# Cross attention: the first query tile is transposed into the bank of the transposed probabilities

## The chip, the cores and the metric

The kernel runs on one core of one Trainium2 chip. The metric is the time of one execution on the device in microseconds. It is given as the median of several runs; the trace comes from one more execution, which was recorded.

## What is computed

One decoder block in float32 on 32 sequences of 64 tokens with 512 features: layer norm and causal self attention, layer norm and cross attention to a context of the same size, layer norm and a feed-forward part with a latent branch, each with its residual. The part that matters here is cross attention:

```python
# cross attention, H = 32 query heads, KVH = 8 key heads, HD = 128, 32 sequences of 64 tokens
q = (hidden_states @ Wq.T).reshape(bsz, q_len, H, HD).transpose(0, 2, 1, 3)
k = (cross_attention_states @ Wk.T).reshape(bsz, kv_len, KVH, HD).transpose(0, 2, 1, 3)
v = (cross_attention_states @ Wv.T).reshape(bsz, kv_len, KVH, HD).transpose(0, 2, 1, 3)
q = _rmsnorm(q, q_norm_w)
k = jnp.repeat(k, GROUPS, axis=1)
v = jnp.repeat(v, GROUPS, axis=1)
k = _rmsnorm(k, k_norm_w)
scores = jnp.einsum('bhqd,bhkd->bhqk', q, k) * scale
scores = scores + attention_mask[:, :, :, :kv_len]
probs = jax.nn.softmax(scores.astype(jnp.float32), axis=-1).astype(q.dtype)
out = jnp.einsum('bhqk,bhkd->bhqd', probs, v)
...
x = x + _L0_attn_ref(_layernorm(x, axis=-1), ...)
x = x + _L0_xattn_ref(_layernorm(x, axis=-1), ctx_4096, mask_1x1xSxS2_ff0, ...)
x = x + _L0_ffn_ref(_layernorm(x, axis=-1), ...)
```

## The kernel before

**Tiling and stages.** The batch is worked off in two halves of 1024 tokens (16 sequences). Each half goes through self attention, cross attention and the feed-forward part. Products of float32 matrices are made from three products of a high and a low part (`split_mm`, lines 358 to 360: hi x hi, hi x lo, lo x hi), so every matrix that is multiplied is first split: ScalarE makes the high part, VectorE or GpSimd the rest.

Cross attention runs over eight turns, one for each key head with its four query heads (`REP` = 4), and in each turn over four chunks of 256 tokens (`CHUNKS` = 4). A turn is one pass of a loop with a register on every engine; the last turn of a half is written out, interleaved with the start of the feed-forward part (`last_turn_and_ffn`). There are 32 chunks in a half and 64 in all.

**What sets the order.** Each engine has its own list of instructions, written out by hand; they meet only at semaphores. `slot(place, k)` on TensorE is one chunk's worth of work, staggered over three chunks: the key and value projection of chunk k + 2 (`project_chunk_kv`, 24 matmuls of 256 columns), the scores of chunk k + 1 (`scores2`), the query projection of chunk k + 2 (`project_chunk_q`, 2 x 12 matmuls of 512 columns), the first output projection of chunk k, the transposed probabilities of chunk k + 1 (`transpose_probs`, into the bank `pt`), the second output projection, the values product of chunk k + 1 (`values2`), and the transposes of keys and queries of chunk k + 2 (`transpose_chunk`). ScalarE's slot follows the same order: copies of keys and values, exponentials, copies of the queries, `evacuate_probs` (line 733: `pt` to `probt`), `transposed_chunk` (lines 846 to 856), and the copy of the values product (`outputs_hi`, line 861). In one chunk of four, two pieces of the next output weights are split between `transposed_chunk` and `outputs_hi` (line 721, and line 1358 on GpSimd); other pieces are split elsewhere in two of the slots.

**The accumulator banks.** PSUM has eight banks here: `acc0` and `acc1`, `sc` for the scores, `pt` for the transposed probabilities, two of `ot` for the values product, `y0` and `y1` for the output projection. The two banks of `acc` are handed out by a running number n: use n goes to bank n % 2. `acc_bank(at, n)` (line 362) waits on TensorE until the use before it of that bank has been read out (`acc_free0` or `acc_free1`), and the last matmul of a use counts up `acc_rdy`, for which the reader waits. A chunk k has six uses, 6k to 6k + 5: keys and values, the two query projections, the transposed keys (`C_KT` = 3), and the two transposed query tiles (`C_QT` = 4 and 5).

`transpose_chunk` (line 539) is ten transposes of 128 x 128: two of the keys (line 544, `acc<-ident,kv`) and four for each query tile (`transpose_tile`, line 376, `acc<-ident,qb`; `qb` is the buffer that holds `qraw` and `q2t`). ScalarE copies the keys with the norm's weights (line 850, `kt<-acc`), then each query tile (line 855, `qb<-acc`). `scores2` waits for both query copies. In the profile a transpose's weight load is an LDWEIGHTS on PEld, and the transpose itself a MATMUL on PE. `scale_chunk` (lines 1087 and 1090 on VectorE) writes the normalised keys and queries that are transposed, after GpSimd's inverse roots (line 1362).

Of the kernel before, what the change touches and what calls it, by code (L numbers as in the profile page):

```python
# [33 lines left out]
CHUNKS = NT // 2  # L34
TURN = 6 * CHUNKS
ACC1 = 4 * NT + 6
# [6 lines left out]
PIECES = [(W_KV, 512), (W_KV + 512, 512), (W_Q, 1024), (W_Q + 1024, 1024), (W_O, 1024), (W_O + 1024, 1024)]  # L43
N_PIECES = 6 + 6 * NG + 8


# [53 lines left out]
def decoder_block(nc, x_in, ctx_in, mask_in, w_self, w_cross, qn_in, kn_in, w_ffn,  # L100
                  f1g_in, expt_in, fc2_in, gamma_in, beta_in, out):
    with ExitStack() as stack:
# [98 lines left out]
        k_sum = count("k_sum", 2, 0, CHUNKS, 0)  # L201
        qk_ve, qk_rs, qk_nrm = (count(n, 0, 0, CHUNKS, 0) for n in ("qk_ve", "qk_rs", "qk_nrm"))
        kbd_done = count("kbd_done", 0, NSEQ, 0, 0)
        vbd_done = count("vbd_done", 0, NSEQ, 0, 0)
# [19 lines left out]
        def use(place, k, j):  # L224


            if k == 0 and j < 3:
                return Place(1, place.half).at, A1[("ckv", "cq0", "cq1")[j]]
            return place.at, 6 * k + j

# [125 lines left out]
        def _(pe):  # L356
# [5 lines left out]
            def acc_bank(at, n):  # L362

                pe.wait_ge(acc_free[n % 2].sem, at(acc_free[n % 2], n // 2))
                return acc[n % 2]
# [173 lines left out]
            def transpose_chunk(place, k):  # L539
                at = place.at  # L540
                pe.wait_ge(qk_nrm.sem, at(qk_nrm, k + 1))
                to = acc_bank(at, 6 * k + C_KT)
                for t in range(2):
                    ins = nc.tensor.transpose(to[:, t * P:(t + 1) * P], kv[:, 2 * (k % CHUNKS) + t, 0:P], ident[:])  # L544
                ins.then_inc(acc_rdy.sem, 1)
                for t in range(2):
                    transpose_tile(at, 6 * k + C_QT + t, qraw[:, 2 * (k % 2) + t].rearrange("p h d -> p (h d)"))

            def scores2(place, k):
                at = place.at  # L550
                evacuated(pe, at, 6 * k + C_QT)
                evacuated(pe, at, 6 * k + C_QT + 1)
                pe.wait_ge(s_add.sem, at(s_add, k))
# [162 lines left out]
        def _(act):  # L716
# [129 lines left out]
            def transposed_chunk(at, k):  # L846
                n = 6 * k + C_KT
                c = k % CHUNKS
                act.wait_ge(acc_rdy.sem, at(acc_rdy, n + 1))
                nc.scalar.mul(kt[:, c * 2 * P:(c + 1) * 2 * P], acc[n % 2][:, 0:2 * P], qkn[:, 2:3]  # L850
                              ).then_inc(acc_free[n % 2].sem, 1)
                for t in range(2):
                    n = 6 * k + C_QT + t
                    act.wait_ge(acc_rdy.sem, at(acc_rdy, n + 1))
                    nc.scalar.copy(q2t[:, k % 2, t], acc[n % 2][:].rearrange("p (h b q) -> p b h q", h=REP, b=2)
                                   ).then_inc(acc_free[n % 2].sem, 1)

# [9 lines left out]
            def slot(place, k, front=True, mid=True, next_group=True):  # L867
# [3 lines left out]
                if next_group and k == 1:  # L871
                    act.wait_ge(acc_rdy.sem, at(acc_rdy, 6 * 3 + C_KV + 1))
                    split_piece(place, 6)
                    split_piece(place, 7)
# [5 lines left out]
                if next_group and k == 1:  # L880
                    act.wait_ge(acc_rdy.sem, at(acc_rdy, 6 * 3 + C_Q + 2))
                    split_piece(place, 8)
# [22 lines left out]
            def last_turn_and_ffn(half):  # L905
# [27 lines left out]
                queries(turn, 3, 0)  # L933
                act.wait_ge(acc_rdy.sem, turn.at(acc_rdy, 6 * 3 + C_KV + 1))
                split_piece(place, 0)
                queries(turn, 3, 1)
                evacuate_probs(turn.at, 2, 0)
                act.wait_ge(acc_rdy.sem, turn.at(acc_rdy, 6 * 3 + C_Q + 2))
                split_piece(place, 1)
# [618 lines left out]
```

## Time and profile before

| | us |
|---|---|
| median of 3 runs | 1846.23 |
| lowest and highest | 1844.5, 1850.87 |
| the profiled execution | 1853.32 |
| its span, first to last instruction | 1851.6 |
| TensorE matmuls busy | 1733.9 (94%) |
| TensorE weight loads busy | 1397.1 (75%) |
| VectorE, ScalarE, GpSimd busy | 941.9, 751.8, 650.7 |

The mean granted clock of TensorE over the span is 0.961. Busy time is the union of an engine's instructions. Matmuls overlap with each other in the records, and a weight load runs while the matmul before it does; so the start times of the weight loads tell more exactly than the busy share when TensorE went on. The profile counts time from the start of the span; cross attention with full slots lies between 234 and 787 us for the first half of the batch, and some 915 us later for the second.

### The profile page before, as it was taken

To read this page: it belongs to the slowest core of one execution; us is meant where nothing else is said; L and a number is where in the kernel's file an instruction comes from. 1 tells how busy PE (TensorE), PEld (TensorE's weight loads), DVE (VectorE), ACT (ScalarE), POOL (GpSimd) and SP (SyncE) were. 2 spreads that over 40 slices of the span, in tenths; PEclk is the share of its full clock that TensorE was granted. 3 is DMA by queue.
4 is the path that set the end of the run, shared out by engine and by line. 5 is a ranking of instruction groups with operands and counts; after the bars stand their busy time and mean duration, and the time that the engine had idled before them with its cause. 6 is when DMAs were issued, how large, how long until landed. Compare 5 with 4: busy or idle time off the path is not lost.

```text
span 1851.6 us, 29634 instructions
## 1 busy us (share of the span) xinstructions
PE 1733.9 (94%) x11352; PEld 1397.1 (75%) x11352; DVE 941.9 (51%) x1657; ACT 751.8 (41%) x1332; POOL 650.7 (35%) x511
## 2 busy tenths in 40 slices
PE   2989899999999999989949998999999999999898
PEld 1745678888888888878937557888888888887797
DVE  3169544444545544474450894545444445456654
ACT  1267444444443434431223763443434444434221
POOL 2188323242323332451012972322332322324410
PEclk8889999999999999999968998999999999999999
DMA  4110010110101101110041100101101101011100
GB/s 154 41 40 18 18 40 19 40 40 17 57 17 40 57 17 45 35 46 18 18 147 31 38 7 18 41 17 40 57 17 40 40 23 51 23 39 47 35 24 23
DMA packets 25871, 70.92 MB, mean 38 GB/s; under 512 B 3152, under 2 KB 3152, under 8 KB 25808
## 3 DMA queue, kind: packets, MB, share of 16 engines
q1 hardware_dynamic: 25808, 70.05, 12.2%
q8 instruction: 43, 0.70, 0.2%
q14 instruction: 20, 0.16, 0.0%
HBM read 65.85 MB, written 4.19 MB: 38 GB/s over the span
## 4 chain that ended last, share of the span: by engine, by line
PE 82%; DVE 6%; ACT 4%; POOL 3%; DMA 2%; issue 2%; SPq 0%; POOLq 0%; DVEq 0%
PE acc L358 14%; PE acc L359 13%; PE acc L360 13%; PE y L358 9%; PE y L360 8%; PE y L359 8%; PE acc L376 4%; PE sc L561 4%; PE ot L575 4%; PE pt L399 2%; ACT kt L850 2%; DMA kv<-in_ctx 2%; PE sc L489 1%; PE acc L544 1%; POOL prob L1371 1%
## 5 line engine op out<-in xcount | busy, mean ns | idle before, releaser
L1358 POOL TENSOR_TENSOR w_lo<-stage,w_hi 128x1024 fp32r<-128x1024 f32 (+1 forms) x88 | 171.2, 1956 | 310.5 <-ACT w_hi L721 310.5
L1371 POOL TENSOR_TENSOR prob<-prob,pmax 128x512 f32<-128x512 f32 x128 | 133.4, 1042 | 355.2 <-DVE pmax L1035 354.9
L358 PE MATMUL y<-w_hi 128*128 128x512 f32 x576 | 236.8, 411 | 0.9 <-issue 0.9
L358 PE MATMUL acc<-w_hi,xn_hi 128*128 128x512 f32 (+1 forms) x576 | 227.0, 394 | 2.9 <-DVE xn_lo L993 2.9
L360 PE MATMUL y<-w_hi,w_lo 128*128 128x512 f32 x576 | 225.7, 392 | 0.0
L359 PE MATMUL y<-w_lo,w_hi 128*128 128x512 f32 x576 | 224.7, 390 | 0.0
L360 PE MATMUL acc<-w_hi,xn_lo 128*128 128x512 f32 (+1 forms) x576 | 219.7, 381 | 0.0
L359 PE MATMUL acc<-w_lo,xn_hi 128*128 128x512 f32 (+1 forms) x576 | 219.5, 381 | 0.0
L993 DVE TENSOR_TENSOR w_lo<-ot,w_hi 128x1024 fp32r<-128x1024 f32 (+1 forms) x80 | 89.3, 1117 | 208.1 <-ACT w_hi L861 207.8
L1377 POOL TENSOR_TENSOR prob<-prob,prec 128x512 f32<-128x512 f32 x128 | 147.8, 1155 | 89.3 <-DVE prec L1043 89.3
L1362 POOL TENSOR_TENSOR qkrs<-qkve,mhalf 128x10 f32<-128x10 f32 x64 | 125.0, 1953 | 152.6 <-DVE qkve L1080 152.6
L729 ACT ACTIVATE prob<-prob 128x512 f32<-128x512 f32 x128 | 81.0, 633 | 188.6 <-POOL prob L1371 187.9
L358 PE MATMUL acc<-w_hi,cx_hi 128*128 128x256 f32 x512 | 154.3, 301 | 0.0
L1074 DVE TENSOR_REDUCE qkss<-kbd 128x4 f32<-128x512 f32 x128 | 87.8, 686 | 119.6 <-ACT kbd L761 116.6
L359 PE MATMUL acc<-w_lo,cx_hi 128*128 128x256 f32 x512 | 147.4, 288 | 0.0
L360 PE MATMUL acc<-w_hi,cx_lo 128*128 128x256 f32 x512 | 146.9, 287 | 0.0
L1040 DVE TENSOR_REDUCE psum_<-prob 128x8 f32<-128x512 f32 x128 | 87.2, 682 | 105.4 <-ACT prob L729 105.2
L358 PEld LDWEIGHTS y<-w_hi 128*128 128x128 f32 x576 | 108.2, 188 | 29.6 <-issue 11.2
L358 PEld LDWEIGHTS acc<-w_hi,xn_hi 128*128 128x128 f32 x576 | 110.4, 192 | 25.7 <-issue 3.6
L1052 DVE TENSOR_TENSOR x<-y,x 128x512 f32<-128x512 f32 x144 | 99.4, 690 | 55.1 <-PE y L360 52.9
L360 PEld LDWEIGHTS y<-w_hi,w_lo 128*128 128x128 f32 x576 | 108.1, 188 | 24.2
L360 PEld LDWEIGHTS acc<-w_hi,xn_lo 128*128 128x128 f32 x576 | 110.4, 192 | 20.9
(129 smaller groups left out, 3685.8 us busy)
## 6 DMA issues: line engine op xcount, KB each, us to landing
stage<-in_w_cross SPq DMA_DIRECT2D x64, 512.0 KB, 3.6
stage<-in_w_cross SPq DMA_DIRECT2D x32, 256.0 KB, 2.7
stage<-in_w_ffn SPq DMA_DIRECT2D x16, 512.0 KB, 3.6
kv<-in_ctx SPq DMA_DIRECT2D x16, 256.0 KB, 3.4
x<-in_x SPq DMA_DIRECT2D x8, 512.0 KB, 7.0
stage<-in_w_self SPq DMA_DIRECT2D x8, 512.0 KB, 3.8
out_x<-x SPq DMA_DIRECT2D x16, 256.0 KB, 2.0
stage<-in_w_self SPq DMA_DIRECT2D x4, 256.0 KB, 7.7
```

The source lines that it names most:

```text
L358: nc.tensor.matmul(target, l_hi, r_hi, start=first, stop=False)
L359: nc.tensor.matmul(target, l_hi, r_lo, start=False, stop=False)
L360: return nc.tensor.matmul(target, l_lo, r_hi, start=False, stop=last)
L729: nc.scalar.activation(prob[:, buffer, :], prob[:, buffer, :], ACT.Exp).then_inc(s_exp.sem, 1)
L993: return nc.vector.tensor_tensor(target, whole, high.bitcast(F32), ALU.subtract)
L1040: nc.vector.tensor_reduce(psum_[:, buffer, :], prob[:, buffer, :].rearrange("p (g k) -> p g k", g=8), AX_X, ALU.add).then_inc(s_sum.sem, 1)
L1052: nc.vector.tensor_tensor(x[:, i % NT, :], y[i % 2][:], x[:, i % NT, :], ALU.add).then_inc(y_free.sem, 1)
L1074: nc.vector.tensor_reduce(qkss[:, k % 2, t * REP:(t + 1) * REP], qsq[:, t], AX_X, ALU.add).then_inc(q_sum.sem, 1)
L1358: nc.gpsimd.tensor_tensor(low, stage[:, place.slot(n), 0:width], high.bitcast(F32), ALU.subtract).then_inc(w_lo_done, 1)
L1362: return nc.gpsimd.tensor_tensor(target, source, mhalf[:, 0:width], ALU.pow)
L1371: nc.gpsimd.tensor_tensor(pr, pr, spread(pmax[:, buffer, :], 8, SEQ), ALU.subtract).then_inc(s_sub.sem, 1)
L1377: nc.gpsimd.tensor_tensor(pr, pr, spread(prec[:, buffer, :], 8, SEQ), ALU.mult).then_inc(s_nrm.sem, 1)
```

## The change

The four transposes of a chunk's first query tile go into the bank `pt` in place of an accumulator bank. Two semaphores are new: `qt_rdy`, counted up by the last of these transposes, and `qt_done`, counted up by ScalarE's copy of the tile. The second query tile stays in an accumulator bank, so a chunk has five uses of them, and `C_QT` is the last. With an odd number of uses, a chunk begins in `acc0` or in `acc1` by turns. `scores2` waits for `qt_done` and for the copy of the second tile. Nothing waits for `pt` ahead of the new transposes: `values2` has waited for the copy of this slot's probabilities. `transpose_probs`, waits and sizes of all else stay as they are. All line numbers below the first edit grow by 3 to 8.

```diff
-TURN = 6 * CHUNKS
+USES = 5
+TURN = USES * CHUNKS
...
+        qt_rdy, qt_done = (count(n, 0, 0, CHUNKS, 0) for n in ("qt_rdy", "qt_done"))
...
@@ def use(place, k, j)
-            return place.at, 6 * k + j
+            return place.at, USES * k + j
...
@@ TensorE: def transpose_chunk(place, k)
-                to = acc_bank(at, 6 * k + C_KT)
+                to = acc_bank(at, USES * k + C_KT)
                 for t in range(2):
                     ins = nc.tensor.transpose(to[:, t * P:(t + 1) * P], kv[:, 2 * (k % CHUNKS) + t, 0:P], ident[:])
                 ins.then_inc(acc_rdy.sem, 1)
-                for t in range(2):
-                    transpose_tile(at, 6 * k + C_QT + t, qraw[:, 2 * (k % 2) + t].rearrange("p h d -> p (h d)"))
+                for h in range(REP):
+                    ins = nc.tensor.transpose(pt[:, h * P:(h + 1) * P], qraw[:, 2 * (k % 2), h], ident[:])
+                ins.then_inc(qt_rdy.sem, 1)
+                transpose_tile(at, USES * k + C_QT, qraw[:, 2 * (k % 2) + 1].rearrange("p h d -> p (h d)"))
@@ TensorE: def scores2(place, k)
-                evacuated(pe, at, 6 * k + C_QT)
-                evacuated(pe, at, 6 * k + C_QT + 1)
+                pe.wait_ge(qt_done.sem, at(qt_done, k + 1))
+                evacuated(pe, at, USES * k + C_QT)
                 pe.wait_ge(s_add.sem, at(s_add, k))
@@ ScalarE: def transposed_chunk(at, k)
-                n = 6 * k + C_KT
+                n = USES * k + C_KT
...
-                for t in range(2):
-                    n = 6 * k + C_QT + t
-                    act.wait_ge(acc_rdy.sem, at(acc_rdy, n + 1))
-                    nc.scalar.copy(q2t[:, k % 2, t], acc[n % 2][:].rearrange("p (h b q) -> p b h q", h=REP, b=2)
-                                   ).then_inc(acc_free[n % 2].sem, 1)
+                act.wait_ge(qt_rdy.sem, at(qt_rdy, k + 1))
+                nc.scalar.copy(q2t[:, k % 2, 0], pt[:].rearrange("p (h b q) -> p b h q", h=REP, b=2)
+                               ).then_inc(qt_done.sem, 1)
+                n = USES * k + C_QT
+                act.wait_ge(acc_rdy.sem, at(acc_rdy, n + 1))
+                nc.scalar.copy(q2t[:, k % 2, 1], acc[n % 2][:].rearrange("p (h b q) -> p b h q", h=REP, b=2)
+                               ).then_inc(acc_free[n % 2].sem, 1)
```

In TensorE's list, the end of the loop's first slot and the beginning of the next, as it was (`acc0` and `acc1` are the two banks, `qb` the queries, `cx_hi` the context in the projection of keys and values):

```order
L575 MATMUL ot<-probt,kv 128x256 [waits ot_lo_done,pt_done]
L575 MATMUL ot<-probt,kv 128x256 x3
L541 REGISTER_ALU
L544 MATMUL acc1<-ident,kv 128x128 [waits acc_free1,qk_nrm]
L544 MATMUL acc1<-ident,kv 128x128
L364 REGISTER_ALU
L376 MATMUL acc0<-ident,qb 128x128 [waits acc_free0]
L376 MATMUL acc0<-ident,qb 128x128 x3
L376 MATMUL acc1<-ident,qb 128x128 [waits acc_free1]
L376 MATMUL acc1<-ident,qb 128x128 x3
L364 REGISTER_ALU
L358 MATMUL acc0<-w_hi,cx_hi 128x256 [waits acc_free0]
```

and as it is with the change:

```order
L581 MATMUL ot<-probt,kv 128x256 [waits ot_lo_done,pt_done]
L581 MATMUL ot<-probt,kv 128x256 x3
L544 REGISTER_ALU
L547 MATMUL acc1<-ident,kv 128x128 [waits acc_free1,qk_nrm]
L547 MATMUL acc1<-ident,kv 128x128
L551 MATMUL pt<-ident,qb 128x128 x4
L367 REGISTER_ALU
L379 MATMUL acc0<-ident,qb 128x128 [waits acc_free0]
L379 MATMUL acc0<-ident,qb 128x128 x3
L361 MATMUL acc1<-w_hi,cx_hi 128x256 [waits acc_free1]
```

The first query tile's four transposes have no wait, the second tile's wait moved from `acc_free1` to `acc_free0`, and the projection of the next keys and values now waits for `acc_free1`, which the copy of the keys counts up.

The same place one slot later, with the change:

```order
L581 MATMUL ot<-probt,kv 128x256 [waits ot_lo_done,pt_done]
L581 MATMUL ot<-probt,kv 128x256 x3
L544 REGISTER_ALU
L367 REGISTER_ALU [waits qk_nrm]
L547 MATMUL acc0<-ident,kv 128x128 [waits acc_free0]
L547 MATMUL acc0<-ident,kv 128x128
L551 MATMUL pt<-ident,qb 128x128 x4
L379 MATMUL acc1<-ident,qb 128x128 [waits acc_free1]
L379 MATMUL acc1<-ident,qb 128x128 x3
L372 REGISTER_ALU
L367 REGISTER_ALU [waits w_lo_done,w_hi_done]
L361 MATMUL acc0<-w_hi,cx_hi 128x256 [waits acc_free0]
```

Here both banks have changed roles: the keys and the next projection share `acc0`, the second query tile has `acc1`.

## Rows read from the trace of the kernel before

**Rows 1.** The page: busy time by engine, and the granted clock in 40 slices.

```profile
PE 1733.9 (94%) x11352; PEld 1397.1 (75%) x11352; DVE 941.9 (51%) x1657; ACT 751.8 (41%) x1332; POOL 650.7 (35%) x511
...
PEclk8889999999999999999968998999999999999999
```

**Rows 2.** The page: the chain that ended last, shares by engine.

```profile
PE 82%; DVE 6%; ACT 4%; POOL 3%; DMA 2%; issue 2%; SPq 0%; POOLq 0%; DVEq 0%
```

**Rows 3.** Waits (us in total, times, longest), and a group of matmuls by line.

```profile
PEld acc L376 <- ACT kt L850: 21.9, 60, 0.4
...
L376 PE MATMUL acc<-ident,qb 128*128 128x128 f32 x512 | 83.1, 289 | 7.7
```

**Rows 4.** Timeline of TensorE's weight loads at a boundary: start us, us, engine, line.

```profile
603.64 0.20 PEld L544 LDWEIGHTS acc<-ident,kv 128*128 128x128 f32 x2 [0.33 <-issue]
603.81 0.47 PEld L376 LDWEIGHTS acc<-ident,qb 128*128 128x128 f32 x4
604.64 0.42 PEld L376 LDWEIGHTS acc<-ident,qb 128*128 128x128 f32 x4 [0.37 <-ACT kt L850]
605.19 0.19 PEld L358 LDWEIGHTS acc<-w_hi,cx_hi 128*128 128x128 f32 x1
```

**Rows 5.** Timeline of ScalarE at the same boundary.

```profile
604.12 0.47 ACT L850 ACTIVATE kt<-acc,qkn 128x256 f32<-128x256 f32 x1 [3.62 <-PE acc L544]
604.55 0.58 ACT L855 COPY qb<-acc 128x512 f32<-128x512 f32 x1
605.34 0.59 ACT L855 COPY qb<-acc 128x512 f32<-128x512 f32 x1 [0.20 <-PE acc L376]
```

**Rows 6.** Weight loads of the first products after the first and the 29th boundary.

```profile
256.22 0.19 PEld L358 LDWEIGHTS acc<-w_hi,cx_hi 128*128 128x128 f32 x1
...
770.49 0.19 PEld L358 LDWEIGHTS acc<-w_hi,cx_hi 128*128 128x128 f32 x1
```

**Rows 7.** Weight loads where the probabilities are transposed, and what follows them.

```profile
617.42 0.59 PEld L399 LDWEIGHTS pt<-ident,prob 128*128 128x128 f32 x4
617.97 0.19 PEld L358 LDWEIGHTS y<-w_hi 128*128 128x128 f32 x1
```

**Rows 8.** The chunk after that boundary: scores, output products, GpSimd, VectorE.

```profile
608.26 1.01 PEld L561 LDWEIGHTS sc<-kt,qb 128*64 128x64 f32 x32
...
614.70 0.19 PEld L358 LDWEIGHTS y<-w_hi 128*128 128x128 f32 x1
...
606.95 4.75 POOL L1358 TENSOR_TENSOR w_lo<-stage,w_hi 128x1024 fp32r<-128x1024 f32 x2 [6.00 <-ACT w_hi L721]
...
614.39 1.05 POOL L1377 TENSOR_TENSOR prob<-prob,prec 128x512 f32<-128x512 f32 x1 [1.70 <-DVE prec L1043]
...
619.62 1.22 DVE L1090 TENSOR_TENSOR qb<-qb,qkrs 128x1024 f32<-128x1024 f32 x1
```

**Rows 9.** The other boundaries: first and second chunk, last chunk of a half.

```profile
214.82 0.29 PEld L544 LDWEIGHTS acc<-ident,kv 128*128 128x128 f32 x2 [2.17 <-DVE qb L1090]
...
217.21 0.29 PEld L358 LDWEIGHTS acc<-w_hi,cx_hi 128*128 128x128 f32 x1 [0.22 <-ACT qb L855]
...
233.94 0.29 PEld L544 LDWEIGHTS acc<-ident,kv 128*128 128x128 f32 x2 [3.42 <-DVE qb L1090]
234.21 1.72 PEld L376 LDWEIGHTS acc<-ident,qb 128*128 128x128 f32 x8
236.16 0.29 PEld L358 LDWEIGHTS acc<-w_hi,cx_hi 128*128 128x128 f32 x1 [0.22 <-ACT qb L855]
...
789.73 0.40 PEld L561 LDWEIGHTS sc<-kt,qb 128*64 128x64 f32 x10 [0.93 <-ACT qb L855]
...
789.07 0.58 ACT L855 COPY qb<-acc 128x512 f32<-128x512 f32 x1 [0.20 <-PE acc L376]
```

**Rows 10.** Busy time of two stretches: length, engines (instructions), clock, DMA.

```profile
233.20:240.00 6.80, 6.06 (x28) 5.72 (x29) 1.91 (x2) 2.56 (x4) 0.00 (x0) 0.50 0.01 2
240.00:814.00 574.00, 567.54 (x3934) 467.86 (x3934) 287.46 (x456) 245.86 (x419) 192.54 (x133) 1.00 0.12 38
```

More of the change, by code:

```diff
@@ L871, in slot @@
                 if next_group and k == 1:
-                    act.wait_ge(acc_rdy.sem, at(acc_rdy, 6 * 3 + C_KV + 1))
+                    act.wait_ge(acc_rdy.sem, at(acc_rdy, USES * 3 + C_KV + 1))
                     split_piece(place, 6)
@@ L880, in slot @@
                 if next_group and k == 1:
-                    act.wait_ge(acc_rdy.sem, at(acc_rdy, 6 * 3 + C_Q + 2))
+                    act.wait_ge(acc_rdy.sem, at(acc_rdy, USES * 3 + C_Q + 2))
                     split_piece(place, 8)
@@ L933, in last_turn_and_ffn @@
                 queries(turn, 3, 0)
-                act.wait_ge(acc_rdy.sem, turn.at(acc_rdy, 6 * 3 + C_KV + 1))
+                act.wait_ge(acc_rdy.sem, turn.at(acc_rdy, USES * 3 + C_KV + 1))
                 split_piece(place, 0)
@@ L937, in last_turn_and_ffn @@
                 evacuate_probs(turn.at, 2, 0)
-                act.wait_ge(acc_rdy.sem, turn.at(acc_rdy, 6 * 3 + C_Q + 2))
+                act.wait_ge(acc_rdy.sem, turn.at(acc_rdy, USES * 3 + C_Q + 2))
                 split_piece(place, 1)
```

## The prediction

> **What bounds the kernel now.** I first read the busy line and the clock line of the page, then the chain of work that ended last, then the waits, and last one boundary between two chunks of cross attention, instruction by instruction. The busy line gives TensorE's matmuls 94% of the span, its weight loads 75%, every other engine 51% or less [rows 1]; the chain that ended last lies on TensorE for 82% of its length [rows 2]. So a microsecond taken out of TensorE's queue in the middle of the kernel is a microsecond of the result, unless something else is late there. The matmul group of the query transposes shows an idle time of only 7.7 us, but the weight loads of the same transposes waited 60 times, 21.9 us in all, for the copy of the keys (line 850) [rows 3].
>
> One boundary shows what that wait is. A chunk ends with ten transposes: two of keys into one accumulator bank, four of the first query tile into the other, four of the second query tile into the first bank again. Their weight loads start at 603.64, 603.81 and 604.64, and the key/value products of the next chunk but one begin at 605.19 [rows 4]. ScalarE copies the keys out from 604.12 to 604.59 and the first query tile from 604.55 to 605.13 [rows 5]. So the second query tile starts 0.05 us after the copy of the keys ends, and the products start 0.06 us after the copy of the first query tile ends: two stalls in a row, each for a bank that has to be read out. From one such boundary to the next it is 18.37 us, the same all through the loop: the products start at 256.22 in the first and at 770.49 in the 29th, and 28 x 18.367 = 514.27 [rows 6]. There are 29 in each half of the batch, 58 in all.
>
> **What the change does to these two stalls.** The first query tile now goes into the bank of the transposed probabilities, which nobody uses at that time: the probabilities of this chunk were copied out before the values product, and those of the next are transposed only after the scores, which wait for the new copy. The second query tile then takes the accumulator bank that the key transposes did not take, last used by the second query projection of this chunk, which was read out before the two output products. It has no reason left to wait. The next products take the bank of the keys, and so wait for line 850's copy instead of for the copy of the first query tile; with five uses a chunk the roles of the two banks alternate, but this order holds in both.
>
> How long the rest takes: four transposes of one group cover 0.47 us, of which 0.14 us is the last load, so they follow each other at (0.47 - 0.14) / 3 = 0.11 us [rows 4]. Then the second tile starts at 603.81 + 4 x 0.11 = 604.25, and the products could start at 604.69. The keys' copy ends at 604.59, and a start 0.05 us behind it is 604.64. That is before 604.69, though only by 0.05 us: the products just don't wait. Against 605.19 that is 0.50 us.
>
> Is the step from transposes to products free of a cost of its own? Where the probabilities' transposes are followed by output products, whose semaphores are long there, the four loads start at 617.42 and the next at 617.97; the last load of the four, counted back from their end (617.42 + 0.59 - 0.14 = 617.87), is 0.10 us before [rows 7]. So the step costs one transpose's pitch, as assumed. At the boundary the same count gives 605.19 - 604.92 = 0.27 us, which is the stall.
>
> 58 x 0.50 = **29.0 us**.
>
> **The six other boundaries.** In the first two chunks of each half TensorE runs at 0.50 of its clock [rows 10], and transposes follow each other at about 0.21 us. First chunk: it starts at 214.82, the products at 217.21 [rows 9]. Eight transposes after a start 0.27 us behind (as in the second chunk, 233.94 to 234.21) give 214.82 + 0.27 + 8 x 0.21 = 216.77, so 0.4 us less. Here the first query tile also loses a wait for VectorE, which only feeds the same 0.4. Second chunk: 234.21 + 8 x 0.21 = 235.89 instead of 236.16, 0.3 us less. Last chunk of each half: its transposes are followed by the scores, which wait for the copy of the second query tile. That copy stood idle 0.20 us for TensorE before 789.07 and now follows the copy before it at once; the scores start 0.2 us sooner than 789.73 [rows 9]. Together 2 x 0.9 = **1.8 us**.
>
> **What is added, and what hides it.** Transposes, copies and bytes are the same in number and size: ten matmuls and three copies a chunk. On TensorE one bank wait of the transposes goes, and the scores' two bank waits become one on the new semaphore and one on a bank. Behind that wait stand the scores and everything after them on TensorE; it is met when the copies are done. They end at 605.93 now (605.34 + 0.59) and at about 605.75 afterwards, since the second follows the first without the 0.20 us; the scores would start at 608.26 - 0.50 = 607.76 [rows 4, 5, 8]. The wait costs nothing with 2 us in hand. The order of ScalarE's queue is unchanged, so nothing is moved past anything on ScalarE, VectorE, GpSimd or the DMA queue.
>
> What comes late next, if TensorE's chunk is 0.50 us shorter? Only chains that cross the boundary lose room, and they begin 0.2 us sooner as well. The worst chunk is the one with two weight pieces behind the copies: GpSimd is busy with them until 606.95 + 4.75 = 611.70, the output products that need them start at 614.70, and the softmax behind them ends at 614.39 + 1.05 = 615.44 against 617.42, when its transposes start [rows 7, 8]. That leaves 3.0 and 2.0 us, of which 0.3 us goes. The scaled queries end at 620.84, against the next key transposes one pitch of 18.37 us behind 603.64, at 622.01: 1.2 us, all inside one chunk, untouched [rows 4, 8]. So I cost all of this at nothing; without the cover of 2.0 us one chunk in four would give back at most its 0.50 us, 16 x 0.50 = 8 us.
>
> **The clock.** In the loop the granted clock is 1.00, the 2.4 GHz level, through 574 us in spite of the stalls; it is 0.50 around 233.2 to 240 us, after TensorE had waited 3.42 us for the scaled queries [rows 9, 10]. A wait that disappears can't bring the lower level into the loop. The stretches at the edges may fall otherwise against the work; one of 6.8 us at half speed costs at most 3.4 us. I take 0 and put 3.4 us on both sides of the range.
>
> **Sum.** 29.0 + 1.8 = 30.8 us. The profiled execution took 1853.3 us with a span of 1851.6, so 1822.5 for it; it lies 7.1 us above the median of the runs, 1846.2, and since the stall is tied to the program and not to a run, I take the same 30.8 us off the median: **1815.4 us**. Own range 1809 to 1822: the runs before spread 6 us, and the clock's 3.4 us stands on either side.
>
> **A reading that would give another number.** By the matmul rows the query transposes were idle for 7.7 us only [rows 3], 0.13 us a boundary, because each matmul's record reaches over the next one's start; the second stall doesn't show there at all. The Trainium skill, in Perfetto Trace Analysis under Identifying the Most-Contended Engine, says that matmul busy share is no good measure of how close TensorE is to its limit, since pipelined instructions overlap, and that the share of weight loads is the one to take. By the matmul rows the sum would be some 7.7 us, by the starts of the loads it is 30.8. I go by the starts: a load that starts 0.06 us after a copy ends is waiting for it.
>
> **The rivals.**
> A: the step from transposes to the next products costs 0.27 us of its own, not 0.11, and only the first stall goes. Each boundary then gives 0.50 - 0.16 = 0.34 us, 58 x 0.34 = 19.7, with 1 us at the edges 1825.5 us. (The step is then the second stall.) For it: 0.27 is what the boundary shows. Against it: the row of the probabilities' transposes [rows 7], and the copy that ends just then. Chance 0.08.
> B: the matmul rows are right and the rest is a pipeline's latency that has to be paid anyway: 7.7 us, 1838.5 us. Against it: both loads start 0.05 and 0.06 us behind the end of a copy. Chance 0.04.
> C: the chunk with weight pieces becomes bound by GpSimd or ScalarE: 8 us less gain, 1823 us. Against it the 2.0 us of room. Chance 0.03.
> D: another wait takes the whole place (the change doesn't do what it says): 1846 us. No row shows a candidate. Chance 0.03.
> E, slower: the products now wait for the keys' copy, with only 0.05 us to spare. If that copy came later than it does, TensorE would wait again, and with it all that follows. The old start is reached when the copy ends at 605.14, 0.55 us later than in the trace, and beyond that each 0.1 us costs 58 x 0.1 = 5.8 us: at 0.65 us, 1852 us. The copy could be late only if ScalarE had something in front of it. Its order is unchanged, and it sat idle before the copy, which starts 0.48 us after the first key transpose [rows 4, 5]. Chance 0.02.
>
> **Chances and range.** Forecast 0.80; A 0.08, B 0.04, C 0.03, D 0.03, E 0.02. A change within 0.3% (5.5 us) can't be told from none here. Faster by more: forecast, A, B and C, 0.95. Within: D, 0.03. Slower: E, 0.02. The range reaches to A, whose condition is the least excluded: 1809 to 1826.
>
> **What the new profile would show.** Weight loads of the key transposes, the first and the second query tile at 0, 0.17 and 0.61 us, the products at 1.05 us; a pitch of 17.87 us instead of 18.37; no wait of the transposes for the keys' copy, and none or some hundredths of a microsecond of the products for it; the scores' wait on the new semaphore without idle time; clock 1.00 in the loop. If the products start at 1.2 us, A was right; at 1.55 us, D. If one pitch in four is longer than the others, C. I would be wrong above all if the keys' copy started later than 0.48 us after the first transpose, since the whole margin there is 0.05 us.

## The result, and the profile after

| | before | after |
|---|---|---|
| median (lowest to highest), 4 runs each | 1846.22 (1844.50 to 1850.87) | 1818.71 (1817.25 to 1819.56) |
| the profiled execution, us | 1853.32 | 1819.56 |
| its span, us | 1851.6 | 1817.8 |
| mean granted clock of TensorE in it | 0.961 | 0.963 |

The profiled execution of the kernel before is one more beside its four; that of the kernel after is the longest of its four.

The ratio is 0.9832, 95% interval 0.9818 to 0.9845: 27.5 us faster, where 30.8 were forecast; 1818.71 lies inside the forecast's own range, 1809 to 1822. The busy line, the clock line and the shares of the chain that ended last, from the page of the kernel after, answer to [rows 1, 2]:

```profile
PE 1708.2 (94%) x11352; PEld 1395.2 (77%) x11352; DVE 942.8 (52%) x1657; ACT 746.0 (41%) x1332; POOL 651.1 (36%) x511
...
PEclk8889999999999999999968898999999999999999
...
PE 84%; DVE 6%; POOL 3%; ACT 2%; DMA 2%; issue 1%; SPq 0%; POOLq 0%; DVEq 0%
```

As many instructions as before, and as much work in the weight loads (1395.2 against 1397.1 us) in a shorter span. ScalarE's share of the chain falls from 4% to 2%: TensorE waits less for its copies.

The boundary of [rows 4, 5] in the kernel after, TensorE's weight loads first (start us, us, engine, line, what; in brackets the idle time before):

```profile
592.95 0.20 PEld L547 LDWEIGHTS acc<-ident,kv 128*128 128x128 f32 x2 [0.33 <-issue]
593.12 0.47 PEld L551 LDWEIGHTS pt<-ident,qb 128*128 128x128 f32 x4
593.56 0.47 PEld L379 LDWEIGHTS acc<-ident,qb 128*128 128x128 f32 x4
593.99 0.19 PEld L361 LDWEIGHTS acc<-w_hi,cx_hi 128*128 128x128 f32 x1
...
597.06 1.01 PEld L567 LDWEIGHTS sc<-kt,qb 128*64 128x64 f32 x32
```

and ScalarE's copies:

```profile
593.43 0.47 ACT L856 ACTIVATE kt<-acc,qkn 128x256 f32<-128x256 f32 x1 [3.62 <-PE acc L547]
593.86 0.59 ACT L859 COPY qb<-pt 128x512 f32<-128x512 f32 x1
594.35 0.59 ACT L863 COPY qb<-acc 128x512 f32<-128x512 f32 x1
```

The loads stand at 0, 0.17, 0.61 and 1.04 us, where 0, 0.17, 0.61 and 1.05 were forecast, against 0, 0.17, 1.00 and 1.55 before. Neither query tile waits any more. The copies of both tiles are done at 594.94, the scores start at 597.06: the scores' wait for the new semaphore is hidden by 2.1 us. In the groups of weight loads (busy us, mean ns | idle us before them), both query tiles now have no idle time at all:

```profile
L379 PEld LDWEIGHTS acc<-ident,qb 128*128 128x128 f32 x256 | 31.8, 148 | 0.0
L551 PEld LDWEIGHTS pt<-ident,qb 128*128 128x128 f32 x256 | 31.5, 146 | 0.0
```

The first products behind the first and behind the 29th boundary, as in [rows 6], give the pitch, (754.67 - 254.78) / 28 = 17.853 us against 18.367:

```profile
254.78 0.19 PEld L361 LDWEIGHTS acc<-w_hi,cx_hi 128*128 128x128 f32 x1
...
754.67 0.19 PEld L361 LDWEIGHTS acc<-w_hi,cx_hi 128*128 128x128 f32 x1
```

Cutting both profiled executions at the first key transpose of a chunk shows where the 33.8 us between them lie:

| from key transpose to key transpose | before | after | difference |
|---|---|---|---|
| start to the first chunk | 214.82 | 215.25 | +0.43 |
| first half: chunks 1 to 3 | 39.85 | 38.49 | -1.36 |
| chunks 3 to 31 (28 pitches) | 514.27 | 499.89 | -14.38 |
| chunk 31 to the last, 32 (1 pitch) | 18.43 | 17.92 | -0.51 |
| last chunk to the second half's first | 341.93 | 341.50 | -0.43 |
| second half: chunks 1 to 3 | 40.05 | 38.43 | -1.62 |
| chunks 3 to 32 (29 pitches) | 532.70 | 517.81 | -14.89 |
| last chunk to the end | 149.55 | 148.55 | -1.00 |

The 58 pitches hold 29.8 us of it, the edges (all the rest) 4.0. The pitches are the same in every trace of one kernel; the edges are not (see The edges, below).

### The profile page after: what moved, and what is told of

Its sections match the earlier page's. It is cut to its first block, busy times and chain, and to the rows that moved or that the text cites. A ratio compares the mean times of both kernels' runs of the same rounds, so it can differ in the third digit from the quotient of the medians.

```text
span 1817.8 us, 29536 instructions
## 1 busy us (share of the span) xinstructions
PE 1708.2 (94%) x11352; PEld 1395.2 (77%) x11352; DVE 942.8 (52%) x1657; ACT 746.0 (41%) x1332; POOL 651.1 (36%) x511
## 4 chain that ended last, share of the span: by engine, by line
PE 84%; DVE 6%; POOL 3%; ACT 2%; DMA 2%; issue 1%; SPq 0%; POOLq 0%; DVEq 0%
PE acc L361 14%; PE acc L363 13%; PE acc L362 13%; PE y L361 9%; PE y L363 9%; PE y L362 8%; PE sc L567 4%; PE ot L581 4%; PE acc L379 3%; PE pt L402 2%; PE pt L551 2%; DMA kv<-in_ctx 1%; PE sc L492 1%; PE acc L547 1%; POOL prob L1379 1%
## 5 line engine op out<-in xcount | busy, mean ns | idle before, releaser
L363 PE MATMUL acc<-w_hi,cx_lo 128*128 128x256 f32 x512 | 145.9, 285 | 0.0
```

Source lines behind the costliest of these rows:

```text
L363: return nc.tensor.matmul(target, l_lo, r_hi, start=False, stop=last)
```

## The experiments

All 11 kernels compute everything; times are medians. Where a line says "the loads", it gives the starts of key transposes, first tile, second tile and next products, counted from the first. The kernel before ran again beside each group: 1850.14 us (20 runs) beside the first four, then 1849.86 (7), 1850.89 (9) and 1850.05 (9).

### Which of the two stalls is worth what

**The bank alone.** The kernel before, with the first query tile written to `pt`, but with every wait and count as it was.

```diff
-                for t in range(2):
-                    transpose_tile(at, 6 * k + C_QT + t, qraw[:, 2 * (k % 2) + t]...)
+                acc_bank(at, 6 * k + C_QT)
+                for h in range(REP):
+                    ins = nc.tensor.transpose(pt[:, h * P:(h + 1) * P], qraw[:, 2 * (k % 2), h], ident[:])
+                ins.then_inc(acc_rdy.sem, 1)
+                transpose_tile(at, 6 * k + C_QT + 1, ...)
```

> The kernel before, with the first query tile transposed into and copied out of the bank of the transposed probabilities, but with its old place in the count of accumulator uses: all waits are those of before. If only the waits count: weight loads at 0, 0.17, 1.00 and 1.55 us after the first key transpose as before, pitch 18.37 us, about 1846 us. If the bank itself is what helps (transposes and copies that don't share two banks): the products earlier than 1.55, down to 1819 us.

Measured: 1850.99 us (1843.69 to 1853.99), ratio 0.9998 (0.9984 to 1.0012). Weight loads at a boundary:

```profile
548.91 0.20 PEld L544 LDWEIGHTS acc<-ident,kv 128*128 128x128 f32 x2 [0.33 <-issue]
549.08 0.47 PEld L548 LDWEIGHTS pt<-ident,qb 128*128 128x128 f32 x4
549.91 0.42 PEld L376 LDWEIGHTS acc<-ident,qb 128*128 128x128 f32 x4 [0.37 <-ACT kt L853]
550.46 0.19 PEld L358 LDWEIGHTS acc<-w_hi,cx_hi 128*128 128x128 f32 x1
```

0, 0.17, 1.00, 1.55 and a pitch of 18.367 us: the old boundary to the hundredth. Another bank is worth nothing by itself; what counts is who waits for whom.

**The first stall alone taken away.** The kernel after, with its products also waiting for the copy of the first tile, as before.

```diff
+                if behind:
+                    pe.wait_ge(qt_done.sem, place.at(qt_done, k))
                 project_kv(*use(place, k, C_KV), k % CHUNKS, cx_hi, cx_lo)
```

> The changed kernel, with one more wait: the key/value products also wait for the copy of the first query tile, as they did before. Only the first stall (second query tile behind the keys' copy) is gone. Serial theory: that copy ends 1.50 us after the first key transpose whatever TensorE does, so the products start at 1.55 as before, pitch 18.37, the second query tile at 0.61; gain about 0, 1845 us. Additive theory, each stall worth its own length: 0.39 us x 58 = 23 us gain, 1823 us.

Measured: 1852.19 us (1848.49 to 1854.34), ratio 1.0012 (0.9999 to 1.0024). Weight loads, and the copy that the products wait for:

```profile
548.51 0.20 PEld L549 LDWEIGHTS acc<-ident,kv 128*128 128x128 f32 x2 [0.33 <-issue]
...
549.12 0.47 PEld L379 LDWEIGHTS acc<-ident,qb 128*128 128x128 f32 x4
550.06 0.19 PEld L361 LDWEIGHTS acc<-w_hi,cx_hi 128*128 128x128 f32 x1 [0.47 <-ACT qb L861]
```

```profile
549.42 0.58 ACT L861 COPY qb<-pt 128x512 f32<-128x512 f32 x1
```

The second tile starts at 0.61, and the products still at 1.55, 0.06 us after the copy ends: what the first wait no longer costs, the second costs in full. One boundary in four has them at 1.73 and one at 1.62, which makes the 58 pitches 3.1 us longer than in the kernel before (the medians are 2.1 us apart); there the added wait stands next to a register or branch instruction in TensorE's list (where exactly the time goes there was not separated).

**The second stall alone taken away.** The kernel after, with the second tile also waiting for the keys' copy.

```diff
+                evacuated(pe, at, USES * k + C_KT)
                 transpose_tile(at, USES * k + C_QT, ...)
```

> The changed kernel, with one more wait: the second query tile waits for the keys' copy, as before. Only the second stall (products behind the first query tile's copy) is gone. Serial theory: second tile at 1.00 us, its four transposes 0.06 + 3 x 0.11, products at 1.39, so 0.16 us a boundary, 58 x 0.16 = 9 us gain, 1837 us. If the step from transposes to products costs 0.27 us of its own: no gain, 1846 us.

Measured: 1839.32 us (1837.28 to 1839.34), ratio 0.9940 (0.9922 to 0.9958).

```profile
544.28 0.20 PEld L547 LDWEIGHTS acc<-ident,kv 128*128 128x128 f32 x2 [0.33 <-issue]
544.45 0.47 PEld L551 LDWEIGHTS pt<-ident,qb 128*128 128x128 f32 x4
545.29 0.42 PEld L379 LDWEIGHTS acc<-ident,qb 128*128 128x128 f32 x4 [0.37 <-ACT kt L857]
545.67 0.19 PEld L361 LDWEIGHTS acc<-w_hi,cx_hi 128*128 128x128 f32 x1
```

The second tile is at 1.01 as before, the products at 1.39 instead of 1.55, so 0.38 us behind it. The four loads are 0.42 us long, 0.14 of it the last: its start is 0.10 us ahead of the products (545.29 + 0.42 - 0.14 = 545.57). That decides rival A: the step from transposes to products is 0.10 us and not 0.27. The pitch is 18.200 at three boundaries of four, so this stall alone is worth 0.167 us there. At the fourth the products start at 1.47 and the pitch is 18.27 to 18.31; over all 58 the gain is 8.7 us, 0.15 a boundary. Nothing for the first stall alone, 0.15 to 0.17 for the second alone, 0.51 for both: they stood in series, and are not a sum.

**The wrong wait.** The kernel after, with its products also waiting for the copy of the second tile: what it would be if the banks had been handed out the other way round.

```diff
+                if behind:
+                    evacuated(pe, place.at, USES * (k - 1) + C_QT)
                 project_kv(*use(place, k, C_KV), k % CHUNKS, cx_hi, cx_lo)
```

> The changed kernel, with one more wait: the products wait for the copy of the second query tile, as they would if the five uses were numbered so that they shared its bank. That copy ends 1.99 us after the first key transpose. If the start of the products follows the copy of the bank's last tenant: products at 2.04 instead of 1.04, pitch 18.85, 58 us more than the changed kernel, 1877 us, slower than before by 31 us. If ScalarE's copies were hidden by then: 1819 us.

Measured: 1885.54 us (1884.57 to 1887.98), ratio 1.0197 (1.0172 to 1.0222).

```profile
557.79 0.20 PEld L549 LDWEIGHTS acc<-ident,kv 128*128 128x128 f32 x2 [0.33 <-issue]
...
558.39 0.47 PEld L379 LDWEIGHTS acc<-ident,qb 128*128 128x128 f32 x4
559.83 0.19 PEld L361 LDWEIGHTS acc<-w_hi,cx_hi 128*128 128x128 f32 x1 [0.96 <-ACT qb L865]
```

The products start at 2.04; the pitch is 18.853, 1.00 us above the kernel after, 58 us in all. The measured distance is 67. The rest lies at the edges, where the first two chunks of a half take 42.5 and 43.3 us instead of 38.5, and where all stretches of granted clock 0.50 add up to 155.8 us instead of 135.0. The expectation had the loop only.

### How near the next wait is

**The keys' copy 0.12 us later.** The kernel after, with a copy of 128 x 32 ahead of it on ScalarE, whose result nobody reads.

```diff
                 act.wait_ge(acc_rdy.sem, at(acc_rdy, n + 1))
+                nc.scalar.copy(delay[:, 0:DELAY], gamma[:, 0:DELAY])
                 nc.scalar.mul(kt[...
```

> The changed kernel with a small extra copy (128x32, SBUF to SBUF) on ScalarE between the wait for the key transposes and the copy of the keys; it makes no part of the output. It delays the keys' copy by d, between 0.1 and 0.3 us. In the changed kernel that copy ends 0.95 us after the first key transpose and the products start at 1.04, a signal takes 0.05. If that wait is the next one: the products start at 1.00 + d and the time grows by 58 x (d - 0.04), 3 to 15 us over the changed kernel. If there were room behind it: no change, 1819 us.

Measured: 1823.55 us (1820.56 to 1823.96), ratio 0.9854 (0.9837 to 0.9870). ScalarE and, behind it, TensorE, whose key transposes began at 558.40:

```profile
558.88 0.22 ACT L858 COPY delay<-gamma 128x32 f32<-128x32 f32 x1 [2.67 <-PE acc L549]
559.00 0.47 ACT L859 ACTIVATE kt<-acc,qkn 128x256 f32<-128x256 f32 x1
```

```profile
559.52 0.19 PEld L363 LDWEIGHTS acc<-w_hi,cx_hi 128*128 128x128 f32 x1
```

The copy ends at 1.07, the products start at 1.12, 0.05 us behind it, as a waiting load does; the pitch is 17.92. So 0.12 us of delay cost 0.07 to 0.08 a boundary, and the remaining 0.04 to 0.05 us is the room that the change left. That is rival E's mechanism, alive and in its place, and the price fits: 58 x 0.08 = 4.6 us, with 5.1 measured against the 1818.4 us of all runs of the kernel after (below); nothing in the kernel sets it off.

**The change again.** The kernel after, unedited.

> The changed kernel again, unedited, beside many runs of the kernel before. If the medians of before differ between calls (1846.2 and 1850.1) only because the mean granted clock of the runs does (0.961 to 0.970), then this kernel is at 1817 to 1820 again and runs of both with the same mean clock differ by 30 to 32 us.

Measured: 1816.40 us (1813.54 to 1821.40), ratio 0.9820 (0.9797 to 0.9842). All 45 runs of the kernel before from the four groups, mean time by the mean granted clock of the run: 0.961, 1853.6 us (4 runs); 0.963, 1850.8 (16); 0.964, 1850.4 (12); 0.965, 1849.2 (6); 0.966, 1848.4 (1); 0.967, 1848.5 (1); 0.968, 1846.6 (3); 0.969, 1845.7 (2). The eight runs of the kernel after: 0.962, 1821.4; 0.963, 1819.3 (2); 0.965, 1818.0 (3); 0.968, 1814.0 (2). At the same clock the two differ by 31.5 us (0.963), 31.2 (0.965) and 32.6 (0.968), and the medians over all runs by 1850.2 - 1818.4 = 31.8.

### What could come next

At the boundary of the kernel after, TensorE steps from the last output product (591.35) to the values product in 0.54 us, and from it to the key transposes with 0.33 us idle:

```profile
591.11 0.19 PEld L362 LDWEIGHTS y<-w_lo,w_hi 128*128 128x128 f32 x1
591.35 0.19 PEld L363 LDWEIGHTS y<-w_hi,w_lo 128*128 128x128 f32 x1
591.89 0.73 PEld L581 LDWEIGHTS ot<-probt,kv 64*128 64x128 f32 x8 [0.35 <-issue]
```

No other engine is named there. In cross attention the values product alone works on 64 rows. The Trainium skill, TensorEngine Tiling (Array Packing), Key Properties, says that changing the tiling mode drains TensorE. These rows fit that, with a step of 0.54 where two products of 128 rows follow each other in 0.24; but no run here separates a drain from whatever else differs at this place.

**The values product moved** between the next projection of keys and values and the scores, and its read-outs with it on ScalarE and VectorE.

```diff
 # TensorE, slot
                 if front:
                     project_chunk_kv(place, k + 2)
+                if back:
+                    values2(place, k)
                 if mid:
                     scores2(place, k + 1)
...
-                if mid:
-                    values2(place, k + 1)
```

> The changed kernel with the values product of chunk k moved from the end of one slot to the next, between the key/value projection and the scores of chunk k+1; its read-out on ScalarE and VectorE moves with it, and the transposes get a wait for the probabilities' copy. The gaps of TensorE's weight loads around it are 0.54, 0.52 and 0.33 us now (before values, values to keys, projection to scores); afterwards 0.23 (output to keys' transposes, as where output and probabilities meet), 0.54 and an unseen one, values to scores, between 0.2 and 0.52. So 0.1 to 0.4 us less a chunk, 6 to 25 us: 1794 to 1813 us. If the scaled queries, which had 1.2 us of room and now lose the 1.06 us of the values product, are late: less, or 0.1 us a chunk lost, 1825 us.

Measured: 1820.79 us (1818.52 to 1824.38), ratio 0.9839 (0.9822 to 0.9855): no better than the kernel after. The pitch changes from boundary to boundary, 17.80 to 17.95 us in the first half of the batch and 17.80 to 17.87 in the second, with means of 17.89 and 17.87. The wait that takes the place (total us, times, longest), the loads, and VectorE's scaling of the queries:

```profile
PEld acc L547 <- DVE qb L1101: 28.0, 36, 5.6
```

```profile
557.79 0.19 PEld L363 LDWEIGHTS y<-w_hi,w_lo 128*128 128x128 f32 x1
558.41 0.20 PEld L547 LDWEIGHTS acc<-ident,kv 128*128 128x128 f32 x2 [0.43 <-issue]
```

```profile
557.07 1.22 DVE L1101 TENSOR_TENSOR qb<-qb,qkrs 128x1024 f32<-128x1024 f32 x1
```

The scaling of the queries ends at 558.29, and the key transposes start 0.12 us later; the profile names no engine for this gap. One boundary earlier it names VectorE, whose scaling (1.22 us from 539.19) ends 0.05 us ahead of the loads:

```profile
540.46 0.20 PEld L547 LDWEIGHTS acc<-ident,kv 128*128 128x128 f32 x2 [0.30 <-DVE qb L1101]
```

At 28 boundaries of the loop the loads start 0.05 us behind the end of the scaling, as here, and at 28 others 0.12 us behind it. So the key transposes wait for the whole of it, though they read only the keys, whose scaling ended earlier (at 557.15).

**The move, and the scaling signalled in three parts**: keys, first query tile, second query tile, with a wait of TensorE for each.

```diff
-                nc.vector.tensor_tensor(keys, keys, ...)
-                nc.vector.tensor_tensor(q, q, spread(qkrs[:, k % 2, 0:2 * REP], ...)).then_inc(qk_nrm.sem, 1)
+                nc.vector.tensor_tensor(keys, keys, ...).then_inc(qk_nrm.sem, 1)
+                for t in range(2):
+                    q = qraw[:, 2 * (k % 2) + t]
+                    nc.vector.tensor_tensor(q, q, ...).then_inc(qk_nrm.sem, 1)
```

> The kernel with the values product beside the scores, and in addition the scaling of the queries split in two instructions with a signal each, so that the key transposes wait for the keys only and each query tile for its own half. In the run with the values product moved, the scaled queries came 0.39 us too late for the transposes (loads 0.62 us after the last output product's where 0.23 is the free step). If that wait was what ate the gain: step 0.23 us, pitch 17.55 instead of 17.85 us, 58 x 0.30 = 17 us less than the changed kernel but for 2 us at the ends, 1803 us. If the values product beside the scores brings nothing by itself: 1819 us.

Measured: 1818.84 us (1815.38 to 1819.67), ratio 0.9826 (0.9812 to 0.9840).

```profile
552.60 0.19 PEld L364 LDWEIGHTS y<-w_hi,w_lo 128*128 128x128 f32 x1
552.82 0.37 PEld L548 LDWEIGHTS acc<-ident,kv 128*128 128x128 f32 x2
```

The step to the key transposes is down to 0.22 us. The pitch is 17.707, where 17.55 was expected: the two key loads are 0.37 us long together instead of 0.20, so the second comes 0.17 us late. The matmuls at the same place show what it follows:

```profile
552.82 0.39 PE L364 MATMUL y<-w_hi,w_lo 128*128 128x512 f32 x1
553.05 0.38 PE L548 MATMUL acc<-ident,kv 128*128 128x128 f32 x2
```

The first key load starts together with the last output product, one matmul ahead of its own. The second starts at 552.82 + 0.37 - 0.14 = 553.05, together with the first key transpose, which follows the product by 0.23 us. Behind the values product the first load and its transpose started together (592.95 in the kernel after), and the second load came 0.06 us later. The four loads of [rows 7], also behind an output product, are 0.59 us long instead of 0.47 in the same way. The expectation took the step of 0.23 us and left this out.

The 58 pitches are 8.0 us shorter (the last one of each half is 18.02), yet the median hasn't moved: from the last chunk to the next half and to the end it now takes 345.0 and 153.9 us, where the kernel after has 341.5 and 148.5. In the last turn (all engines, the rows that matter):

```profile
765.47 3.44 DVE L1105 TENSOR_TENSOR qb<-qb,qkrs 128x512 f32<-128x512 f32 x2
...
765.95 2.42 POOL L1374 TENSOR_TENSOR w_lo<-stage,w_hi 128x1024 fp32r<-128x1024 f32 x1
...
768.97 0.62 PEld L380 LDWEIGHTS acc<-ident,qb 128*128 128x128 f32 x4 [2.27 <-DVE qb L1105]
```

and the stretch behind that wait (length; busy us of PE, PEld, DVE, ACT, POOL; granted clock; DMA):

```profile
769.10:772.50 3.40, 3.40 (x22) 2.25 (x24) 1.32 (x3) 1.04 (x2) 0.00 (x0) 0.50 0.47 154
```

The scaling of one tile, 0.68 us elsewhere, takes 2.84 us there, as long as GpSimd splits a weight piece beside it. TensorE waits 2.27 us, and then goes through 3.4 us at 0.50 of its clock.

**The signals in three parts alone.** The kernel after with the second edit only.

> The changed kernel with only the scaling split in two and its three signals. There the scaled queries are 1.2 us early, so the split can bring nothing: pitch 17.85, 1819 us. If the split helps by itself: less than 1815 us. If a third VectorE instruction a chunk costs: over 1822 us.

Measured: 1819.40 us (1818.65 to 1820.98), ratio 0.9836 (0.9821 to 0.9851), pitch 17.855: nothing. There was no wait for the scaled queries in the loop that it could shorten.

**The scaling ahead of the statistics in the last turn**, on top of both edits, so that it is over when GpSimd's split begins.

```diff
                 final_statistics(0)
-                final_statistics(1)
                 scale_chunk(turn.at, 3)
+                final_statistics(1)
```

> The kernel with the values product beside the scores and the scaling split in two, and in the last turn of each half the scaling stands ahead of the second tile's layer norm statistics on VectorE. In the run without this, the loop's pitch was 17.71 us (0.15 below the changed kernel's, 8.5 us in 58), yet the total was equal: in the last turn the second half of the scaling took about 2.7 instead of 0.68 us while GpSimd split a weight piece (2.42 us), TensorE waited 2.3 us for it in each half, and the granted clock fell to 0.5 for 3.4 us behind it. With the scaling 1 us earlier, before GpSimd's piece: the two waits and their clock stretches go, 1808 to 1811 us. If the loss at the ends has another cause: 1819 us.

Measured: **1812.34 us** (1809.03 to 1813.41), ratio 0.9791 (0.9778 to 0.9805): the fastest kernel here, 37.7 us ahead of the kernel before in the same group, and 6.6 us ahead of the next kernel, which ran beside it and is the kernel after but for one order (interval 0.9818 to 0.9848). VectorE and GpSimd at that place:

```profile
765.27 1.29 DVE L1105 TENSOR_TENSOR qb<-qb,qkrs 128x512 f32<-128x512 f32 x2
...
768.09 3.04 DVE L1027 TENSOR_SCALAR xn<-x,mv,rstd 128x512 f32<-128x512 f32 x2
768.18 2.67 POOL L1374 TENSOR_TENSOR w_lo<-stage,w_hi 128x1024 fp32r<-128x1024 f32 x1
```

Both tiles are scaled in 1.29 us, and no transpose of queries waits. The split now meets the layer norm, which takes 3.04 us for two tiles, and that moves TensorE's wait to a later place instead of ending it: VectorE makes the low part of the values product only behind the layer norm, until 772.26, and the output products that read it start 0.08 us later.

```profile
771.05 1.21 DVE L1007 TENSOR_TENSOR w_lo<-ot,w_hi 128x1024 fp32r<-128x1024 f32 x1
...
772.34 0.19 PEld L362 LDWEIGHTS y<-w_hi 128*128 128x128 f32 x1 [2.25 <-issue]
...
773.40:776.80 3.40, 3.40 (x10) 2.52 (x9) 3.12 (x11) 1.56 (x2) 2.12 (x3) 0.51 0.08 33
```

This wait of 2.25 us is there in both halves, and half speed behind it too, so the expectation that waits and clock stretches go was wrong in its mechanism, though the time, 1812.3 where 1808 to 1811 were expected, came close. What was gained: these output products start 6.2 us behind the last chunk's first key load, where it was 8.8 in the run without the order (and 4.2 in the kernel after). The last chunk to the next half and to the end takes 342.1 and 151.3 us, still 3.3 us more than in the kernel after.

**That order alone.** The kernel after with the third edit only.

> The changed kernel with only the scaling of the last chunk ahead of the second tile's statistics. There the last key transposes wait 0.4 us less: 0.40 us idle for the scaled queries before them, twice. 0 to 1 us gain, 1818 us. If the order alone makes the better version's gain: 1810 us.

Measured: 1818.89 us (1816.64 to 1820.38), ratio 0.9833 (0.9818 to 0.9848): nothing. The order only repairs part of what the two other edits had broken at the ends.

## Why the prediction was right

**The two stalls.** Forecast 0.50 us a boundary, 29.0 in all; measured 0.513, 29.8. The loads stand where they were forecast to a hundredth. That both stalls were there, and in series, was read from two starts 0.05 and 0.06 us behind the end of a copy [rows 4, 5]; the runs with one stall alone taken away, 0 and 0.15 us a boundary, show that the two don't add up. The waits for the keys' copy of [rows 3], 21.9 us, would have been 8 us too few, and taking away that wait alone gained nothing.

**By which rows.** The matmul group's idle time of 7.7 us [rows 3] forecast 1838.5; the kernel took 1818.7. The starts of the weight loads decide. The Trainium skill, Perfetto Trace Analysis, Identifying the Most-Contended Engine, says that the matmul busy share is no good measure of how close TensorE is to its limit, and names the arithmetic done against the peak and the share of the weight loads instead. This pair agrees: the matmul busy share stayed at 94% while 2% of the span went, and that of the weight loads rose from 75% to 77%.

**The margin.** Forecast 0.05 us between the start that the loads allow and the one that the keys' copy allows; the delayed copy shows 0.04 to 0.05. The copy still starts 0.48 us after the first key transpose.

**The edges.** Forecast 1.8 us. Where it was forecast it is there: in the first and second chunk of a half the products start 1.98 us behind the first key load instead of 2.39 and 2.22, so 0.41 and 0.24 us less, where 0.4 and 0.3 were forecast. The scores of the last chunk start 2.06 us behind it instead of 2.36, where 2.16 was forecast: two copies that follow each other on ScalarE start 0.48 to 0.49 us apart, though each is recorded as 0.58 or 0.59. That makes 1.9 us in both halves.

The profiled pair has 4.0 us at the edges, but that number is partly luck. Outside the 58 pitches the kernel after takes 782.2 us in its first trace and 781.0 in its second; the kernel before takes 786.2, and the run with the bank alone, whose boundaries are the same, 784.8. By the pair that is chosen the edges give 2.6 to 5.2 us. What is more than 1.9 goes with the clock, for which 0 was taken with 3.4 us either way: the stretches at 0.50 add up to 145.9 and 139.0 us in the two old ones, and to 135.0 and 129.8 in the two new ones. Whether the change shortens them or they fall so by chance, two traces a side can't tell. The kernel after's counterpart of the first line of [rows 10], and of the second:

```profile
233.20:237.60 4.40, 3.20 (x15) 3.21 (x16) 1.14 (x2) 1.83 (x4) 0.00 (x0) 0.61 0.02 4
238.00:800.00 562.00, 559.37 (x3953) 470.41 (x3952) 289.56 (x458) 243.27 (x420) 194.79 (x133) 1.00 0.13 39
```

The granted clock is 0.50 from 234.2 to 237.6 us, 3.4 us instead of 6.8, and the same happened at two other places (1148 and 1735 us in the kernel before); in its second trace one of these three is 6.8 us long again. In the loop it is 1.00, as forecast.

**Why 27.5 and not 30.8.** In the mechanism nothing is missing: the loop gives more than forecast, not less. The forecast took its gain off a median of 1846.2 us, of three runs. The kernel before's four runs, 1844.5 to 1850.9, lie low within the 45 that were taken beside the experiments, whose median is 1850.2; against these the gain is 31.8 us, which is the loop's 29.8 and the 1.9 found at the edges. So the term that was off is the base, by some 4 us, and not a term of the sum. That the clock made those four runs short is likely but not shown, for their clock isn't on record. The profiled pair misses on the other side, with 33.8 us.

**The rivals.** A (a step of 0.27 us) fell with the second stall taken away alone, and with the kernel after itself: the step is 0.10 us in both (593.56 + 0.47 - 0.14 = 593.89, and the products at 593.99). B (the matmul rows) fell with the result. C (weight pieces) is not to be seen: the pitch is the same all through the loop, and no wait of the output products has come up. D (another wait takes the place) is excluded by the start of the products at 1.04; that such a thing can happen here shows in the run with the first stall alone taken away, where the second took over all of it. E (the keys' copy late) has its mechanism confirmed by the delayed copy and its condition not met.

## What to carry to other kernels

Two waits in a row for two copies of one engine are one chain: one alone was worth 0 or 8.7 us here, both 29.8. Work out each new start from the start of the weight loads and the end of the copy, not from summed waits. When a bank changes hands, look at whose copy the next user now waits for: here waiting for the first copy left 0.04 us to spare, and waiting for the third cost 67 us against that. Before work is moved next to other work, look at the loads inside a group and not only at the step to its first: with the values product moved, that was 0.17 us of the 0.30 us expected. After a gain in the loop, look at the written-out ends, where an order that was harmless can meet another engine's work.

## What the runs showed of the hardware

- **VectorE beside GpSimd.** The same scaling of 128 x 512 took 0.68 us alone and 2.84 us beside a 2.42 us split on GpSimd; with the order changed, the layer norm beside a 2.67 us split took 3.04 us for two tiles. The Trainium skill, GPSIMD Engine Reference, Key points, says that GpSimd shares its SBUF interfaces with VectorE, in contention with VectorE instructions that have two SBUF inputs or run in a 2-port mode. The first case agrees (two inputs in SBUF); for the second the rows show the delay and not the mode.
- **The clock follows waits at the ends.** In the last turn a wait of 2.27 us was followed by 3.4 us at 0.50 of the clock, and with the order changed a wait of 2.25 us, at another place, by 3.4 us at 0.51. The kernel after has no wait longer than 1.0 us there, and its clock stays at 1.00 until 804 us. Added waits of 1 us at each boundary left the loop's pitch at exactly 1.00 us more, while the half-speed stretches outside grew from 135.0 to 155.8 us in all.
- **Runs differ by their clock.** From a mean granted clock of 0.969 down to 0.961 the kernel before goes from 1845.7 to 1853.6 us, about 0.9 us for each 0.001. Two medians of four runs of the kernel after are 2.3 us apart (1818.7 and 1816.4).
- **The same wait is not equally dear everywhere.** With the first stall alone taken away, the products started at 1.62 and 1.73 us instead of 1.55 at two of four boundaries, and with the second alone at 1.47 instead of 1.39 at one of four. A register or branch instruction of TensorE stands at the first two; that it is the cause was not tried.
